# Axis stages of a scan network: products in 384 columns taken off VectorE, front matmuls dealt out singly

## What is computed

```python
x1, res = split(x @ in_w.T); x1 = silu(conv1d(x1, conv_w))
delta = softplus(x1 @ xproj_w[:6].T @ dproj_w.T + dproj_b); B, C = x1 @ xproj_w[6:].T
c = exp(min(suffix_cumsum(delta * A), 15))
y = sum_n(C[n] * cumsum(delta * x1 * B[n] * c[:, n]) / (c[:, n] + 1e-6)) + x1 * D
out = (y * silu(res)) @ out_w.T
```

## Time and profile before

| what | us |
|---|---|
| median of 3 runs | 17351.04 |
| lowest and highest | 17338.99, 17353.57 |
| profiled execution | 17346.37 |
| its span, first to last instruction | 17344.5 |
| VectorE busy in the span | 15921.2 (92%) |
| TensorE matmul busy | 15345.0 (88%) |
| ScalarE busy | 15021.8 (87%) |
| GpSimd busy | 14270.5 (82%) |

### The profile page before, as it was taken

How to read it: one execution, slowest core, us unless ns; L and a number is a source line. 1 busy time by engine, 2 the same in 40 slices (tenths; PEclk the granted TensorE clock), 3 DMA queues, 4 the chain that set the end, 5 groups by cost and what they waited for, 6 DMA issues and landing times. The chain is left out here.

```text
span 17344.5 us, 317054 instructions
## 1 busy us (share of the span) xinstructions
PE 15345.0 (88%) x72568; PEld 9862.9 (57%) x72568; DVE 15921.2 (92%) x42443; ACT 15021.8 (87%) x26177; POOL 14270.5 (82%) x11720
## 2 busy tenths in 40 slices
PE   8888999999999999999799999998998999997788
PEld 3335666666666666666566666666666666663233
DVE  7999999999999999999899999999999999996799
ACT  7768999999998999999799999999989999894588
POOL 4668888888888888888788888888888888886677
PEclk9999999999999999999899999999999999998899
DMA  2004444444444444444344444444444444443000
GB/s 42 16 18 73 83 83 82 84 83 81 82 83 82 83 83 84 83 80 82 67 84 83 83 84 83 82 81 83 83 81 86 82 81 82 83 82 58 20 15 14
DMA packets 1146585, 1251.52 MB, mean 72 GB/s; under 512 B 919521, under 2 KB 938621, under 8 KB 1144701
## 3 DMA queue, kind: packets, MB, share of 16 engines
q0 software_dynamic: 202752, 1006.72, 30.5%
q1 hardware_dynamic: 938596, 221.43, 10.4%
q10 hardware_dynamic: 3352, 2.14, 0.1%
HBM read 152.05 MB, written 71.35 MB: 13 GB/s over the span
## 5 line engine op out<-in xcount | busy, mean ns | idle before, releaser
L1509 POOL TENSOR_TENSOR h_sm<-h_sm,h_wr 128x768 f32<-128x768 f32 x1536 | 3004.8, 1956 | 201.4 <-DMA h_held<-h_sent 96.9
L1509 POOL TENSOR_TENSOR w_sm<-w_sm,w_wr 128x768 f32<-128x768 f32 x1536 | 2992.2, 1948 | 152.9 <-DVE w_wr L1247 86.1
L1709 PE MATMUL w_pz<-w_xr,w_tri 128*128 128x384 f32 x6144 | 2725.1, 526 | 385.0 <-DVE w_sent L1247 166.5
L1709 PE MATMUL h_pz<-h_xr,h_tri 128*128 128x384 f32 x6144 | 2710.9, 523 | 369.2 <-DVE h_sent L1247 166.6
L1531 POOL TENSOR_TENSOR w_cbuf<-w_cbuf,w_dxs 128x384 f32<-128x384 f32 x2176 | 2369.0, 1124 | 763.2 <-ACT w_cbuf L1373 739.3
L1531 POOL TENSOR_TENSOR h_cbuf<-h_cbuf,h_dxs 128x384 f32<-128x384 f32 x2176 | 2367.0, 1126 | 725.4 <-ACT h_cbuf L1373 700.3
L1373 ACT ACTIVATE w_cbuf<-w_pe_e 128x1024 f32<-128x1024 f32 x2304 | 2366.2, 1027 | 604.5 <-PE w_pz L1705 366.7
L1373 ACT ACTIVATE h_cbuf<-h_pe_e 128x1024 f32<-128x1024 f32 x2304 | 2370.2, 1029 | 548.4 <-PE h_pz L1705 314.5
L1396 ACT ACTIVATE w_rbuf<-w_pe_e 128x1024 f32<-128x1024 f32 x2304 | 2372.6, 1030 | 65.4 <-DVE w_wr L1247 57.1
L1396 ACT ACTIVATE h_rbuf<-h_pe_e 128x1024 f32<-128x1024 f32 x2304 | 2373.3, 1030 | 53.1 <-DVE h_wr L1247 45.7
L1247 DVE SCALAR_TENSOR_TENSOR w_wr<-w_pz,w_bct,w_rbuf 128x192 f32<-128x192 f32 x6144 | 2208.1, 411 | 152.9 <-POOL w_sm L1509 93.3
(11 more groups left out here) (383 smaller groups left out, 30646.8 us busy)
## 6 DMA issues: line engine op xcount, KB each, us to landing
h_held<-h_sent POOLq DMA_DIRECT2D x576, 768.0 KB, 5.8
w_held<-w_sent POOLq DMA_DIRECT2D x576, 768.0 KB, 5.9
h_lt<-pieces_s SPq DMA_DIRECT2D x512, 96.0 KB, 7.1
h_held<-h_held POOLq DMA_DIRECT2D x128, 384.0 KB, 4.0
w_lt<-pieces_s SPq DMA_DIRECT2D x512, 96.0 KB, 7.8
w_held<-w_held POOLq DMA_DIRECT2D x128, 384.0 KB, 4.0
pieces_s<-h_pieces SPq DMA_DIRECT2D x384, 48.0 KB, 2.1
pieces_s<-w_pieces SPq DMA_DIRECT2D x384, 48.0 KB, 2.1
```

What stands on the lines that cost most here:

```text
L1509: tt(sm[:, g], sm[:, g], wr[:, RINGED.index((g, u)) % 3], ALU.add).then_inc(s_add, 1)
L1709: t.matmul(pz[:, P % 2, 0:2 * DX], tri[:], x, start=True, stop=True).then_inc(s_z, 1)
```

## The change

The change does four things in `phase_axis`.

1. `WIDE` becomes empty. 36 pairs are OTHER (3, 5 and 7 of every chunk, so pairs 3 and 35 are new) and 60 go by halves. The scaled pairs fall from 48 to 36.
2. The bias matmul of the fronts is cut into three of 128 columns, and the front matmuls are dealt to new steps, mostly one to a step.
3. GpSimd's order: LEAD goes from 8 to 10, so the three products of a chunk come one unit earlier. Each send has its own unit. Its waits come ahead of the products of that unit, and the send follows the first of them, ahead of the unit's add, where it followed the add.
4. Several front operations move by a step or more, among them STEPS_U 17 to 16, RESID_U 37 to 44, PREFIX_P 38 to 40, GATE_P 82 to 93, HELD_AT 33 to 31, TREE_AT 36 to 38 and O_CH 8 to 7.

```diff
-        X_BIAS, DT_BIAS = 2, 19
-        X_SLOTS = {3: (0,), 4: (1,), 5: (2,), 6: (3,), 7: (4,), 8: (5,), 9: (6, 7), 10: (8, 9), 11: (10,), 12: (11,)}
-        DT_SLOTS = {20: (0, 1), 21: (2,), 22: (3,), 23: (4,), 24: (5,), 25: (6,), 26: (7,), 27: (8,)}
-        BC_SLOTS = {36: (0,), 37: (1,), 38: (2,), 39: (3,), 40: (4, 5)}
-        Y_SLOTS = {52: (0, 1), 53: (2, 3), 54: (4,), 55: (5,)}
-        O_SLOTS, Z_SLOTS = (59, 60, 61), (75, 76, 77)
-        XS_CH, SX_CH, DT_CH, LOG_CH, BC_CH, P1_CH, P2_CH, O_CH, SZ_CH = 0, 1, 3, 3, 5, 5, 6, 8, 9
-        STEPS_U, SUFFIX_U, REST_U, PIECE_U, RESID_U = 17, 20, 25, 28, 37
-        XC_P, PREFIX_P, GATED_P, GATE_P = 17, 38, 57, 82
-        LESS, PLAIN, MORE = [35], [33], [3, 2, 82]
-        OTHER = [P for P in range(4, PAIRS) if P % 8 in (3, 5, 7) and P not in LESS]
-        WIDE = [P for P in range(PAIRS) if P % 8 == 1 and P not in PLAIN] + MORE
+        X_SLOTS = (1, 2, 3, 4, 5, 6, 6, 7, 8, 9, 10, 10, 11, 12, 13)
+        DT_SLOTS = (17, 19, 20, 21, 21, 23, 23, 25, 26, 26, 27, 28)
+        BC_SLOTS = (34, 35, 36, 37, 38, 39)
+        Y_SLOTS = (51, 51, 52, 52, 54, 54)
+        O_SLOTS, Z_SLOTS = (58, 59, 59), (75, 75, 76)
+        XS_CH, SX_CH, DT_CH, LOG_CH, BC_CH, P1_CH, P2_CH, O_CH, SZ_CH = 0, 1, 3, 3, 5, 5, 6, 7, 9
+        STEPS_U, SUFFIX_U, REST_U, PIECE_U, RESID_U = 16, 20, 24, 28, 44
+        XC_P, PREFIX_P, GATED_P, GATE_P = 16, 40, 56, 93
+        OTHER = [3, 5, 7, 11, 13, 15, 19, 21, 23, 27, 29, 31, 35, 37, 39, 43, 45, 47, 51, 53, 55, 59, 61, 63, 67, 69, 71, 75, 77, 79, 83, 85, 87, 91, 93, 95]
+        WIDE = []
...
-        THIRD, LEAD = (1, 2), 8
+        THIRD, LEAD = (1, 2), 10
...
-        FOLD_AT = ((1, 3), (1, 22))
-        HELD_AT, TREE_AT = (33, 49), (36, 50)
+        HELD_AT, TREE_AT = (31, 49), (38, 50)
...
+        SEND_AT = ((6, 10, 14, 18, 22), (30, 34, 38, 42))
+        FOLD_AT = (27, 46)
...
+                def ready_to_send(T, g, b):
+
+                    n = sent_no(g, b) - 1
+                    if not (isinstance(T, int) and T == 0 and n == 0):
+                        pool.wait_ge(s_da, T * 16 * ND + n * 16)
+                    if b is not None:
+                        pool.wait_ge(s_wd, T * PAIRS + g * 48 + 4 * b + 6)
...
-                        for P in OTHER:
-                            if max((P - LEAD) // 2, 0) == U:
-                                product(T, P)
+                        due = [x[1:] for x in SENDS if x[0] == U]
+                        made = [P for P in OTHER if max((P - LEAD) // 2, 0) == U]
+                        assert len(due) < 2 and (made or (g, u) in RINGED or not due)
+                        if due:
+                            ready_to_send(T, *due[0])
+                        if made:
+                            product(T, made[0])
+                        if due and made:
+                            send(*due[0])
+                        for P in made[1:]:
+                            product(T, P)
                         if (g, u) in RINGED:
                             add(T, g, u)
-                        if (g, u) in CARRIER:
-                            send(*CARRIER[g, u])
+                        if due and not made:
+                            send(*due[0])
...
-                def front_bias(f, row):
+                def front_bias(f, row, j):
...
-                    t.matmul(pf[:, 0:JB * TB], brow[:, row, :], ones[:].rearrange("r j t -> r (j t)"), start=True,
+                    t.matmul(pf[:, j * TB:(j + 1) * TB], brow[:, row, :], ones[:, j, :], start=True,
```

More of the change, by code:

```diff
@@ L918, in phase_axis @@
         KEPT = [[u for u in range(UN) if u // 2 not in SENT[g]] for g in range(2)]
-        FOLD_AT = ((1, 3), (1, 22))
-        HELD_AT, TREE_AT = (33, 49), (36, 50)
+        HELD_AT, TREE_AT = (31, 49), (38, 50)
         RINGED = [(g, u) for g in range(2) for u in KEPT[g][1:]]
[L922 to L928, removed]
+        SEND_AT = ((6, 10, 14, 18, 22), (30, 34, 38, 42))
+        FOLD_AT = (27, 46)
+        SENDS = sorted([(U, g, b) for g in range(2) for b, U in zip(SENT[g][1:], SEND_AT[g])] +
+                       [(FOLD_AT[g], g, None) for g in range(2)])
+        BLOCKS = [x for x in SENDS if x[2] is not None]
+        assert all(b is None or U >= g * UN + 2 * b + 1 for U, g, b in SENDS)
         SUMS = []
@@ L938, in phase_axis, with block_no, sent_no @@
         NA, ND = len(SUMS), len(SENDS)
+        def block_no(g, b):
+            return [x[1:] for x in BLOCKS].index((g, b))
+        def sent_no(g, b):
+            return [x[1:] for x in SENDS].index((g, b)) + 1
         def summed(what, g, n):
@@ L1211, in place @@
                     k, at = SENT[g].index(u // 2), u % 2 * 4 + at
-                    return held[:, g, at, :] if k == 0 else sent[:, BLOCKS.index((g, u // 2)) % 2, at, :]
+                    return held[:, g, at, :] if k == 0 else sent[:, block_no(g, u // 2) % 2, at, :]
                 def room(T, g, u):
@@ L1501, in add @@
                 def add(T, g, u):
-                    if (g, u) in CARRIER:
-                        n = SENDS.index(CARRIER[g, u])
-                        if not (isinstance(T, int) and T == 0 and n == 0):
-                            pool.wait_ge(s_da, T * 16 * ND + n * 16)
                     pool.wait_ge(s_wd, T * PAIRS + g * 48 + 2 * u + 4)
@@ L1518, in add_held @@
                 def add_held(T, g):
[L1520 removed]
+                    pool.wait_ge(s_da, T * 16 * ND + sent_no(g, None) * 16)
                     pool.wait_ge(s_add, T * NA + NA + ahead("held", g, 0))
@@ L1709, in sums @@
                         t.matmul(pz[:, P % 2, 0:2 * DX], tri[:], x, start=True, stop=True).then_inc(s_z, 1)
-                front_bias(0, 0)
+                for j in range(JB):
+                    front_bias(0, 0, j)
                 for k in range(4 * JB):
                     in_proj(0, 0, k)
-                front_bias(1, 1)
+                for j in range(JB):
+                    front_bias(1, 1, j)
                 for k in range(JB * JB):
@@ L1763, in _ @@
-                        if not first:
-                            for k in Y_SLOTS.get(P, ()):
-                                turn_y(T - 1, x1, base + f_at["Y"], k)
-                            if P in O_SLOTS:
-                                out_proj(base + f_at["O"], O_SLOTS.index(P))
-                        if not last and P in Z_SLOTS:
-                            gate_proj(F, base + f_at["Z"], Z_SLOTS.index(P))
+                            for k in range(5 * JB):
+                                if X_SLOTS[k] == P and k % 5 == 0:
+                                    front_bias(base + f_at["X"], 0, k // 5)
+                                elif X_SLOTS[k] == P:
+                                    in_proj(F, base + f_at["X"], k // 5 * 4 + k % 5 - 1)
@@ new lines, in _ @@
+                            for k in range(4 * JB):
+                                if DT_SLOTS[k] == P and k % 4 == 0:
+                                    front_bias(base + f_at["DT"], 1, k // 4)
+                                elif DT_SLOTS[k] == P:
+                                    dt_proj(x3, k // 4 * 3 + k % 4 - 1)
+                            for k in range(2 * JB):
+                                if BC_SLOTS[k] == P:
+                                    bc_proj(x3, base + f_at["BC"], k)
@@ new lines, in _ @@
+                        if not first:
+                            for k in range(2 * JB):
+                                if Y_SLOTS[k] == P:
+                                    turn_y(T - 1, x1, base + f_at["Y"], k)
+                            for j in range(JB):
+                                if O_SLOTS[j] == P:
+                                    out_proj(base + f_at["O"], j)
+                        if not last:
+                            for j in range(JB):
+                                if Z_SLOTS[j] == P:
+                                    gate_proj(F, base + f_at["Z"], j)
```

22 lines of the change are left out of this document (5 added, 17 removed).

## The result

The changed kernel takes 17951.39 us (median of 4 runs, 17943.21 to 17956.01) where the kernel before takes 17351.04 us beside it (median of three runs; a fourth took 31823.63 us and is left out): 1.0347 times as long, 95% interval 1.0327 to 1.0368. That is 600 us, or 4.7 us in each of the 128 bodies, and lies outside my range. The forecast was no change.

A forecast was written before the change was run, and what follows sets the result against it. No engine was taken as full; VectorE, the fullest, loses idle time in short waits. Terms 174 - 218 - 275 + 154 + 154 = -11 us gave 17335 against the profiled 17346.4, so median 17340 us, no change; range 17180 to 17530.

The forecast's parts named there:

- (a): VectorE's products: fourteen of 384 columns go, twelve pairs by halves come; +1.36 us a body, +174 us in all.
- (b): Front matmuls: bias in parts ends pair 5's wait and other waits for sums shrink; -1.7 us a body, -218 us.
- (c): Earlier sends nearly end pair 80's DMA wait, and the ring waits for GpSimd's adds go; -2.15 us a body, -275 us.
- rival C: GpSimd's backlog at a body's end keeps the ring waits and delays pair 3; +1.8 us a body, 17580 us, chance 0.16.
- (d): Pair 3, now GpSimd's, waits behind its chain of products and adds, longer in w; mean +1.2 us a body, +154 us.
- (e): Chunk 3: a third scaled pair's triangles on ScalarE delay step 33's fill, lengthening pair 35's wait; +1.2 us, +154 us.
- rival D: Other waits of the same length take over, so only VectorE's extra 174 us show; 17525 us, chance 0.14.

The follow-up runs named there:

- e6: The changed kernel with VectorE's scan at step 34 instead of 40; 17689.1 us, 1.0198 times the kernel before.
- e10: The kernel before with the new front (matmul slots, bias in parts, moved front operations), but the scan at step 34; 17322.5 us, 0.9984.
- e9: The kernel before with only the scan moved, from step 38 to 34; 17202.1 us, 0.9918.
- e11: The changed kernel with the w stage's residual back at unit 37 from 44; 17862.5 us, 1.0288.
- e13: The kernel before, scan at step 34, bias in parts, front matmuls doubled only where no fill stands, Y, O, Z, O_CH, GATED_P as changed; 17256.9 us, 0.9950.
- e3: The kernel before with only GpSimd's new order, LEAD, HELD_AT and TREE_AT of the change; 17371.4 us, 1.0014.
- e7: The changed kernel with pair 3 by halves on VectorE, no longer on GpSimd; 17677.7 us, 1.0192.
- e2: The kernel before with only the new OTHER and WIDE lists; 17832.1 us, 1.0282.
- e5: The kernel before with only the new front: matmuls dealt to new slots, bias in three parts, front operations moved; 17776.3 us, 1.0252.
- e15: The changed kernel with pair 35 by halves on VectorE, no longer on GpSimd; 17965.1 us, 1.0353.
- e14: The changed kernel with the scan at step 34, the residual at unit 37 and pair 3 by halves on VectorE; 17463.0 us, 1.0068.
- e16: The kernel before with the scan at step 34 and the sends placed as in the change, LEAD 8, held and tree as before; 17142.1 us, 0.9883.
- e17: The kernel before, scan at step 34, changed send places, X's new slots, bias in parts, Y, O, Z, O_CH, GATED_P as changed; 17058.2 us, 0.9831.
- e12: The changed kernel with GpSimd's order within a unit as before: products, the send's DMA wait, add, send; 17902.7 us, 1.0314.
- e8: The kernel before with only the scan moved, from step 38 to 40; 17653.7 us, 1.0179.

## Why the prediction was wrong, by its own steps

**Not in the sum: the scan.** I listed PREFIX_P 38 to 40 among the things that move and gave it no term. A VectorE operation's duration I took as its own, and that one operation has two inputs in SBUF. The direct lengthening is (1900 - 1233 + 2178 - 1348) / 2 = 0.75 us a body by the means of its rows in both stages, 96 us. The step as it now stands costs 262 us against step 34 (e6). This is the first failed step, and it is shown: one number, +310 and -142 us in the kernel before. It is not the largest. The kernel before paid 142 us for its own step against step 34, so what the change added by the scan is 262 - 142 = 120 us of the 600.

**(a) VectorE's work, forecast +1.36 us: right.** Of the 2.0 us of busy time, 0.75 are the scan, and 1.24 are left.

**(b) Front matmuls, forecast -1.7 us: wrong.** The bias wait of 0.74 went where the front is changed alone (in the changed kernel pair 5 still waits 0.4 us in h in the mean), but e10 against e9 shows the front with a price of 0.9 us a body, 112 us where I forecast -218. It lies in w, where the residual is, and e11 prices the residual's unit at 0.7 in the changed kernel; that it is as much here was not tried. In h the front nets about nothing: I took each wait as separate, but VectorE, coming sooner, waits for the sums at pairs 9 and 13 in its place (e13, with other slots, has 0.3 us at pair 9), and DT's tail in steps 26 to 28 goes with 0.6 us more at pairs 28 to 31.

**(c) DMA and ring, forecast -2.15 us: half wrong.** Alone (e3) this part measured +24 us where I forecast -275. The DMA wait went, as said (piece 80-83 fell by 1.46 and 0.77 us; less the gate's 0.47 and with the 0.19 for pair 82 put back it is -1.2 in h and -0.5 in w). The ring wait, forecast to go, grew from 1.18 to 1.31 us a body in h and from 1.45 to 1.95 in w; the rest of 84-copy's rise is the gate (0.47), pairs 89 and 1 by halves (0.38) and smaller waits. The chain from unit 42 does not start when VectorE is ready for it: I left out the DMA wait, now ahead of products, and the tree's unit, which lies at the same place. Add 42 starts 4.3 us after weighting 85 in h and 5.0 in w, where it started 2.1 and 2.4 us after it before. It was my rival C (16%), with its sign. Its mark "pair 3 waits over 2 us and the ring waits are there still" is met in w.

**(d) Pair 3, forecast +1.2 us: mis-sized.** The mechanism is as I gave it; the size is 2.8 us (e7: 274 us are 2.1 a body, and 0.65 for the product that came in its place), the residual's share in w and the shorter scan within it. I had let the chain start with chunk 11's c groups. They do end as pair 84 begins, but GpSimd comes to their products only 2.1 us later in h and 2.9 in w, behind that same backlog (0.7 and 1.1 with its old order, e2). From there to the product of pair 3 it is 15.7 us in h, where I had 15.4. The lower clock after the wait, about 0.9 us a body in pairs 4 to 7, had no term at all.

**(e) Pair 35, forecast +1.2 us: right in size, half right in cause.** The wait grew from 1.19 to 2.28 us, near the 2.4 that I gave. In the mean of 63 bodies in h it is 1.3 us before, 2.6 with the new lists alone (e2), 1.9 with the new front alone (e5), 2.5 in the changed kernel and 1.7 in e15. So 0.65 of the growth is the product that VectorE no longer makes there, as I said. The other 0.6, which I put on the third pair's triangles, comes with the lists alone, though e2 changes all lists, and it comes with the front alone; with both it comes once, and taking pair 35 back then gains nothing (e15). What in the front does it stays open. e10 has the longer piece 32-35 (6.73 us), e13 hasn't (6.00); between the two lie the DT slots that end at 28 and 27, the BC slots, STEPS_U and XC_P, among others.

e14 stands 114 us above the kernel before, fewer than (a)'s 159 (1.24 x 128) because its scan is hidden.

The stated rule of rival D (VectorE, the fullest engine, gets the work) pointed to the right side, but its 174 us are under a third of what came.

## What to carry to other kernels

Before moving an operation in a hand-written order, look at the spread of its durations (minimum, median, maximum): an operation whose median is over its minimum may be held up by something that shows no wait, as the scan was here. Its best place was a wait of its own engine: in e9, e16 and e17 it costs next to nothing there, even where it still takes 1.6 us. Don't sum gains of waits on engines that follow each other closely: a gain counts only as far as the next producer or transfer is ready, so the late transfer is moved first (e16) and the front after it (e17). A consumer right behind the other engine's longest chain (pair 3) waits for all of that chain, and it did so with either order of the sends (e2, e12). A wait of TensorE can also cost more than its length, as the granted clock may be lower for the pairs behind it.

## What the runs showed of the hardware that I had not expected

- A scan over 128x384 with both inputs in SBUF takes 0.96 us undisturbed, and up to 4.1 us beside GpSimd's operations, with no wait in the records: the time stands in the instruction's own duration. It can stand through two GpSimd operations in a row (e8), though in the changed kernel it ended 0.8 us after the first of two adds (the scan takes 2.07 us at 4628.67, the first add 2.09 at 4627.83). What decides between the two was not tried.
- It goes the other way as well: `make_dx` took 1.71 us in place of 1.00 where the scan came 0.05 us earlier (e9), and two adds beside the scan took 4.52 us in the changed kernel:

```profile
4627.83 4.52 POOL L1510 TENSOR_TENSOR h_sm<-h_sm,h_wr 128x768 f32<-128x768 f32 x2
4632.31 0.82 POOL L1486 TENSOR_TENSOR h_ab<-h_sf 128x384 f32<-128x384 f32 x1
```

  Two adds without it took 3.99 us.
- After waits of TensorE of the same length, 1.4 us, the granted clock was at 1.2 GHz in one body and at 2.4 in the next, and the same four sums took 1.57 and 0.91 us. The 31 matmuls of pairs 4 to 7 then took 7.16 and 4.78 us.
